# Attention in groups of four heads: the next group's scores and maxima between this group's transposed scores and values

## The reference

```
layer 0:  xn = layernorm(x)
          s  = a recurrence over time with gates (h = tanh(h A + u Bm), y = g (h C' + u D') + (1 - g) xn) W_out + b_out + xn
          g  = silu(tanh(xn wo' + c uo' + bo)),  c from a second recurrence
          x  = x + s * g
layer 1:  xn = layernorm(x)
          q, k, v = xn Wq', xn Wk', xn Wv'            16 heads of 16, scaled by 1/16
          scores  = q k' / 4, causal;  weight = softmax(scores);  s = (weight v) Wproj' / 16
          d2 = squared distances of xn to 32 prototypes; the nearest 2 are chosen, with softmax weights
          g  = silu(sum over the 2 of weight * (A (B xn) + bias))    rank 16
          x  = x + s * g
```

## Time and profile before

| | us |
|---|---|
| median of 3 runs | 1231.76 |
| lowest and highest | 1228.45 and 2604.05 |
| the profiled execution | 1227.31 |
| its span, first to last instruction | 1225.5 |
| first scores of batch 0 | at 456.3 |
| one round of the loop over batches | about 97 |
| mean granted clock of TensorE | 0.936 |

### The profile page before, as it was taken

One profiled execution on the slowest core, in us unless ns is written; L12 is line 12 of the kernel. 1 busy time (PEld: TensorE's weight loads), 2 busy tenths in 40 slices (PEclk: granted clock), 3 DMA queues, 4 the chain that ended last, 5 costly groups with the idle time before them and its releaser, 6 DMA issues.

```text
span 1225.5 us, 20586 instructions
## 1 busy us (share of the span) xinstructions
PE 1069.8 (87%) x6848; PEld 708.9 (58%) x6848; DVE 510.6 (42%) x1028; ACT 488.5 (40%) x1198; POOL 256.6 (21%) x237
## 2 busy tenths in 40 slices
PE   4699999999997557898799799889889889979986
PEld 2267777777775334555555565555555545546644
DVE  4611211212122233644744743653663564565461
ACT  2334444444444202263263264255246336326234
POOL 2200101101004223222321420521322322422000
PEclk8899999999998768899899999989989989989989
DMA  6530101011030075058039019119308506705700
GB/s 212 174 102 29 51 26 51 29 48 49 28 111 18 34 107 99 19 100 159 18 77 181 18 59 153 46 52 129 94 35 128 112 18 112 145 18 93 96 19 18
DMA packets 80501, 93.99 MB, mean 77 GB/s; under 512 B 9920, under 2 KB 72032, under 8 KB 80480
## 3 DMA queue, kind: packets, MB, share of 16 engines
q1 hardware_dynamic: 76256, 89.52, 35.1%
q10 hardware_dynamic: 4224, 4.19, 1.0%
HBM read 59.84 MB, written 33.59 MB: 76 GB/s over the span
## 4 chain that ended last, share of the span: by engine, by line
PE 70%; DVE 10%; issue 7%; ACT 5%; DMA 4%; SPq 2%; POOL 1%; DVEq 0%; ACTq 0%; POOLq 0%
PE PS L708 22%; PE PS L844 5%; PE PS L781 5%; PE PS L922 5%; PE PS L887 5%; DVE nm L1451 5%; PE PS L865 3%; PE PS L695 3%; PE PS L811 3%; PE PS L759 3%; DMA XT<-xt_d 2%; PE PS L948 2%; PE PS L790 2%; PE PS L889 2%; ACT arena L1184 2%
## 5 line engine op out<-in xcount | busy, mean ns | idle before, releaser
L708 PE MATMUL PS<-arena 128*128 128x256 f32 x1024 | 312.1, 421 | 0.0
L1451 DVE TENSOR_REDUCE nm<-PS 128x2 f32<-128x256 f32 (+3 forms) x256 | 200.9, 817 | 90.3 <-PE PS L867 89.3
L695 PEld LDWEIGHTS PS<-arena 128*72 128x72 f32 x1024 | 129.9, 141 | 68.1 <-ACT arena L1069 4.6
L1069 ACT ACTIVATE arena<-PS 64x8 f32<-64x8 f32 x512 | 88.5, 173 | 185.1 <-PE PS L695 181.4
L708 PEld LDWEIGHTS PS<-arena 128*128 128x128 f32 x1024 | 155.5, 192 | 0.0
L865 PE MATMUL PS<-K,Q 96*128 96x128 bf16 (+3 forms) x512 | 129.8, 319 | 25.0 <-DVE nm L1451 20.5
L1184 ACT ACTIVATE arena<-PS 128x1024 f32<-128x1024 f32 x128 | 128.5, 1029 | 29.2 <-PE PS L889 28.6
L887 PE MATMUL PS<-Q,K 98*128 98x512 bf16 (+3 forms) x512 | 122.8, 318 | 16.6 <-DVE nm L1451 14.1
L1311 DVE SCALAR_TENSOR_TENSOR arena<-arena 128x512 f32<-128x512 f32 x16 | 11.1, 694 | 267.7 <-ACT arena L1080 267.7
L695 PE MATMUL PS<-arena 128*72 128x8 f32 x1024 | 121.3, 191 | 0.0
L867 PE MATMUL PS<-negmask,identb 128*128 128x128 bf16 x512 | 105.6, 228 | 0.0
(11 more groups left out here) (161 smaller groups left out, 1399.9 us busy)
## 6 DMA issues: line engine op xcount, KB each, us to landing
qk_d<-QB SPq DMA_DIRECT2D x24, 512.0 KB, 2.9
Q<-qk_d SPq DMA_DIRECT2D x96, 128.0 KB, 8.9
K<-qk_d SPq DMA_DIRECT2D x96, 128.0 KB, 9.5
X<-in_L_attn_x SPq DMA_DIRECT2D x12, 512.0 KB, 13.5
arena<-xt_d SPq DMA_DIRECT2D x16, 256.0 KB, 3.2
gt_d<-arena SPq DMA_DIRECT2D x16, 256.0 KB, 2.5
wx_d<-arena SPq DMA_DIRECT2D x16, 256.0 KB, 2.0
XT<-xt_d SPq DMA_DIRECT2D x8, 512.0 KB, 9.9
```

Of the source, the lines that this page charges most:

```text
L695: pe.matmul(PS[0:WIDE, 7, 0:B], w_ab, HB[:, step], start=True, stop=True).then_inc(c_mm.sem, 1)
L708: mm = pe.matmul(o, lhs, rhs, start=first, stop=last)
L1451: v_.tensor_reduce(nm[:, i, 2 * hp:2 * hp + 2], PS[:, 2 * (u % 3):2 * (u % 3) + 2, 0:(i + 1) * P], AX.X, ALU.max, negate=True).then_inc(m_ ...
```

## The change

Heads go in four groups of four, and a batch is four stages. In stage g TensorE makes the transposed scores of group g in ten units of one bank each, two banks in turn (3 and 4), and between them the scores of the next group in eleven units of one bank each, three banks in turn (0 to 2); group 0 of batch b + 1 is done in stage 3 of batch b. Bank 5 keeps the values, banks 6 and 7 all side steps, now the projection too. The side steps of batches b - 1, b + 1 and b + 2 are spread over the stages. VectorE takes maxima with a reduction for each unit of 512 columns or less, turns into one small piece of 16 rows by 128 per group, writes the scaled values itself (`value`), and does the splits after the maxima of stage 1; ScalarE takes exponentials 512 columns at a time. In DRAM query and key now lie as part, q or k, dimension, head, token; a group's operands are read in six transfers, each of 3, 2 or 1 blocks of 16 rows of four heads (4 KB), where the blocks of the query repeat one part. Before the loop, loads for batch 0 are followed on SP's queue by those for batch 1, and then by the first maxima.

```diff
-PAIRS = [(0, 0), (0, 1), (1, 0), (0, 2), (2, 0), (1, 1)]
+PAIRS = [(0, 0), (0, 1), (0, 2), (1, 0), (1, 1), (2, 0)]
+BLOCKS = [(0, 3), (3, 2), (5, 1)]
 KS = len(PAIRS) * HD
 KM = KS + 2
 SCORE_SCALE = float(D) ** -1.0 * float(HD) ** -0.5
@@ -31,7 +32,13 @@
 P_AT = {0: 0, 1: 512, 3: 896, 2: 1024}
 PU = P_AT[2]
-TU = 3 * H // 2
+G = 4
+GH = H // G
+ROWS = [(3, 0, 1), (3, 1, 1), (3, 2, 1), (3, 3, 1), (2, 0, 1), (2, 1, 1), (2, 2, 1), (2, 3, 1), (1, 0, 2), (1, 2, 2),
+        (0, 0, 4)]
+SU = len(ROWS)
+TQ = 5 * GH // 2
+TU = G * TQ
 PW = NT * (NT + 1) // 2 * P
 BIG = 1.0e30
...
-        qk_d = nc.dram_tensor("qk_d", (SPLIT, 2, D, T), BF16, kind="Internal").ap()
+        qk_d = nc.dram_tensor("qk_d", (SPLIT, 2, HD, H, T), BF16, kind="Internal").ap()
...
+            def save_operands(b, n):
+                if n == 0:
+                    sp.wait_ge(q_ld[G - 1].sem, q_ld[G - 1].at(b, 0))
+                    hold()
+                sp.wait_ge(q_s.sem, q_s.at(b, (2, 5, 6)[n]))
+                for c in range(2):
+                    for m in range(KT):
+                        sp.dma_start(qk_d[n, c, :, m * H // 2:(m + 1) * H // 2].rearrange("d h t -> h d t"),
+                                     QB[:, n, c * KT + m]).then_inc(q_st.sem, 16)
...
+            def load_operands(b, g, after):
+                sp.wait_ge(q_st.sem, q_st.at(b, 2 * KT * SPLIT))
                 hold()
-                if before is not None:
-                    sp.wait_ge(t_mm.sem, t_mm.at(before, (a + 1) * TU // 2))
+                if after:
+                    sp.wait_ge(t_mm.sem, t_mm.at(b - 1, (g + 1) * TQ))
                     hold()
-                rows_of = slice(a * D // 2, (a + 1) * D // 2)
-                heads = slice(a * H // 2, (a + 1) * H // 2)
-                for r, pair in enumerate(PAIRS):
-                    for c, dst in enumerate((Q6, K6)):
-                        sp.dma_start(dst[r * HD:(r + 1) * HD, heads, :],
-                                     qk_d[pair[c], c, rows_of].rearrange("(h d) t -> d h t", d=HD)
-                                     ).then_inc(q_ld[a].sem, 16)
-            def take_maxima(b, a):
-                sp.wait_ge(m_h.sem, m_h.at(b, a + 1))
-                heads = slice(a * H // 2, (a + 1) * H // 2)
-                sp.dma_start(Q6[KS:KS + 1, heads, :], nmh[:, a]).then_inc(m_ld[a].sem, 16)
-                sp.dma_start(Q6[KS + 1:KS + 2, heads, :], nml[:, a]).then_inc(m_ld[a].sem, 16)
-            def batch(b, more):
-                if more:
-                    load_batch(b + 1)
-                take_maxima(b, 0)
+                heads = slice(g * GH, (g + 1) * GH)
+                for at, n in BLOCKS:
+                    first = PAIRS[at][0]
+                    rows_of = slice(at * HD, (at + n) * HD)
+                    sp.dma_start(Q6[rows_of, heads, :],
+                                 qk_d[first:first + 1, 0, :, heads].broadcast_to([n, HD, GH, T])
+                                 ).then_inc(q_ld[g].sem, 16)
+                    sp.dma_start(K6[rows_of, heads, :], qk_d[0:n, 1, :, heads]).then_inc(q_ld[g].sem, 16)
+            def take_maxima(b, g):
+                sp.wait_ge(m_h.sem, m_h.at(b, g + 1))
+                heads = slice(g * GH, (g + 1) * GH)
+                for row, part_of in ((KS, nmh), (KS + 1, nml)):
+                    sp.dma_start(Q6[row:row + 1, heads, :].rearrange("o h (i q) -> o (h i) q", q=P), part_of[:, g]
+                                 ).then_inc(m_ld[g].sem, 16)
...
+            def stage1(b, more, more2):
+                if more2:
+                    load_rows(b + 2)
+                    load_gates(b + 2)
+                take_maxima(b, 2)
+                if more:
+                    save_operands(b + 1, 0)
+            def stage2(b, more):
+                if more:
+                    save_operands(b + 1, 1)
+                    save_operands(b + 1, 2)
+                    load_operands(b + 1, 0, True)
+                    load_operands(b + 1, 1, True)
+                take_maxima(b, 3)
+            def stage3(b, more):
+                if more:
+                    load_operands(b + 1, 2, True)
+                    take_maxima(b + 1, 0)
...
+            def scores(b, g, u):
+                i, h, n = ROWS[u]
+                bank = u % 3
+                if u == 0:
+                    pe.wait_ge(q_ld[g].sem, q_ld[g].at(b, 2 * len(BLOCKS)))
+                elif u == 2:
+                    pe.wait_ge(m_h.sem, m_h.at(b, g))
+                elif u > 2:
+                    pe.wait_ge(m_r.sem, m_r.at(b, g * SU + u - 2))
+                w = (i + 1) * P
+                for e in range(n):
+                    pe.matmul(PS[:, bank, e * w:(e + 1) * w], Q6[0:KS, g * GH + h + e, i * P:(i + 1) * P],
+                              K6[0:KS, g * GH + h + e, 0:w], start=True, stop=False)
+                    mm = pe.matmul(PS[:, bank, (e + 1) * w - P:(e + 1) * w], identb[:, :], negmask[:, :],
                                    start=False, stop=True)
                 mm.then_inc(m_mm.sem, 1)
-            def maxima_turn(b, a, more):
...
+            def turned(b, g, k):
+                if k == 0:
+                    pe.wait_ge(m_ld[g].sem, m_ld[g].at(b, 2))
+                pe.wait_ge(t_e.sem, t_e.at(b, g * TQ + k - 1))
+                h, bank = g * GH + k // 5 * 2 + k % 5 // 2, 3 + k % 2
+                if k % 5 == 4:
+                    turned_tile(b, h - 2, 2, bank, 0)
+                    mm = turned_tile(b, h - 1, 2, bank, 2 * P)
+                elif k % 5 % 2 == 0:
+                    mm = turned_tile(b, h, 0, bank, 0)
+                else:
+                    turned_tile(b, h, 1, bank, 0)
+                    mm = turned_tile(b, h, 3, bank, 3 * P)
...
+            def stage(b, g, side, nxt):
+                for k in range(TQ):
+                    turned(b, g, k)
+                    if nxt is not None:
+                        for u in (2 * k, 2 * k + 1):
+                            if u < SU:
+                                scores(*nxt, u)
+                        if k == 7:
+                            maxima_turn(*nxt)
+                    run(side, k)
...
+            def stage2(b, more):
+                side = {0: [], 1: [lambda: values(b, 1)], 2: [], 3: [lambda: values_turn(b, 1)]}
+                for n, k in enumerate((0, 2, 3, 4, 5, 6, 7, 8)):
+                    side.setdefault(k, []).append(lambda n=n: experts(b, n, more))
+                stage(b, 2, side, (b, 3))
...
+            def maxima(b, g, u):
+                i, h, n = ROWS[u]
+                dve.wait_ge(m_mm.sem, m_mm.at(b, g * SU + u + 1))
+                v_.tensor_reduce(nm[:, g, h:h + n, i],
+                                 PS[:, u % 3, 0:n * (i + 1) * P].rearrange("p (n w) -> p n w", n=n), AX.X, ALU.max,
                                  negate=True).then_inc(m_r.sem, 1)
...
+            def stage(side, nxt):
+                for u in range(SU):
+                    if nxt is not None:
+                        maxima(*nxt, u)
                     for step in side.get(u, ()):
                         step()
-                maxima_low(b, 1)
+                if nxt is not None:
...
+            def stage1(b, more, first=False):
+                side = {6: [lambda: divide(b, 0)]}
+                if not first:
+                    side[1] = [lambda: add_rows(b - 1)]
+                stage(side, (b, 2))
                 if more:
                     split(b + 1, 0, Q)
                     remainder(b + 1, 0)
@@ -1502,25 +1658,31 @@
                     split(b + 1, 1, Q)
                     remainder(b + 1, 1)
                     split(b + 1, 2, Q)
-                    value(b + 1, 0)
-                    value(b + 1, 1)
-                    split(b + 1, 1, K)
-                divide(b, 0)
-                if more:
-                    split(b + 1, 2, K)
                     distance(b + 1)
-                divide(b, 1)
-                if more:
-                    odds_apart(b + 1)
-                    choose(b + 1)
-                divide(b, 2)
-                if more:
-                    weigh(b + 1, 0)
-                    weigh(b + 1, 1)
-                divide(b, 3)
-                if more:
-                    weigh(b + 1, 2)
-                finish(b)
+            def stage2(b, more):
+                side = {6: [lambda: divide(b, 1)]}
+                if more:
+                    side[1] = [lambda: split(b + 1, 1, K)]
+                    side[5] = [lambda: odds_apart(b + 1)]
+                    side[7] = [lambda: split(b + 1, 2, K)]
+                    side[8] = [lambda: choose(b + 1)]
+                side[10] = [lambda: gate(b, 0)]
+                stage(side, (b, 3))
+                gate(b, 1)
```

More of the change, by code:

```diff
@@ L455, in batch, with stage0 @@
+            def stage0(b, more, first=False):
+                if not first:
+                    load_x1(b - 1, more)
+                    load_operands(b, 3, True)
                 if more:
@@ L1009, in _ @@
```

(26 more changed lines are left out.)

715 lines of the change are left out of this document (396 added, 319 removed).

## The result

The changed kernel takes 1460.6 us (median of four, 1458.3 to 1468.5) against 1230.1 before: a ratio of 1.190, 95% interval 1.185 to 1.195. One of the four executions of the kernel before took 2604 us and is left out of the ratio. I had forecast slower, by the right mechanism, with 1410 us and a range up to 1455; the time lies just above it. The profiled execution is the slowest of the four, 1468.5 with a span of 1466.6.

What follows compares the result with a forecast made beforehand. TensorE, with gaps made by waits, was taken to bound the kernel; 81 us of work plus waits and low clock gave a 118.5 us period, and with prologue and last batch 1410 us. Range 1215 to 1455, the forecast's own 1370 to 1455.

Steps and rivals of the forecast that it cites:

- Step 1: VectorE's maxima 28 us a batch (26 before), ScalarE's exponentials about 3 us more, all hidden under TensorE: zero on the sum.
- Step 2: Maxima chain, now four times a period: TensorE waits of 0, 1.4 and 2.5 us behind stages 0, 1 and 3.
- Step 3: Low-rank rounds in stage 3: TensorE waits 2.0 us (0 to 4) for VectorE multiplications standing behind two maxima.
- Step 4: VectorE's 9.9 us block at the end of stage 1: TensorE stands 6.1 us in stage 2 for an unread bank.
- Step 5: Operand loads on 3 and 2 engines in stage 2 hold back group 3's maxima: 18.5 us wait in seven periods.
- Step 6: TensorE's low clock, from gaps of 6 and 18 us: 7 us lost a period (3 to 9), 4.9 before.
- 81: TensorE's own work per batch at 2.4 GHz, in us, taken as the base of the period.
- the 118.5: Forecast period of the batch loop in us, the sum of TensorE's work, waits and low clock, against 97.25 before.
- Loads on 16 engines: Rival: block count does not matter to loads; period 100 to 109, time 1257 to 1337, middle 1295 us; chance 0.17.
- The fed case: Rival, first four steps of stage 2: fast loads, VectorE's block ends in time; period 90.5, 1183 us; chance 0.12.
- The worse case: Rival: loads on few engines also delay SP's issues, so stage 0's maxima come late; over 1455 us; chance 0.05.

Runs made afterwards that it cites:

- interleaved source: Changed kernel with each operand load's source walked with its 16 dimensions outermost and its 3 or 2 blocks inside: 1315.6 us, ratio 1.072.
- the second experiment: Changed kernel with each block of 16 rows loaded as a transfer of its own, 12 per group: 1344.6 us.
- the mended kernel: Changed kernel with loads' 16 dimensions outermost, last cast earlier, VectorE's distances behind it, SP's order and the order before the loop altered: 1209.9 us, ratio 0.987.

## Why the prediction was right in kind and wrong in size

1. **Step 1, sizes:** right. VectorE 55 us a round (52.6 and 2), ScalarE 41 to 43, both hidden.
2. **Step 2, maxima chain:** 1.17 and 1.63 for 1.4 and 2.5, right, the second smaller. But the 0 behind stage 0 is 1.6 to 2.6 in five rounds: the maxima of group 1 go out 7.3 us behind the last load of group 3 and need 5.0 us to land (787.81 to 792.84) instead of 1.7. With interleaved loads this wait is gone, so it is the loads again, in a place where I had put nothing.
3. **Step 3, low rank:** 2.2 for 2.0. Right.
4. **Step 4, VectorE's block:** 5.5 for 6.1. Right.
5. **Step 5, loads in stage 2: the step that failed, by size.** The wait is 25.5 for 18.5. The mechanism is shown by experiment: the engine count by the interleaved source and its marks, the place in the queue by the maxima put first. The count from VectorE's block on (687.3) was 23.6 us to the first load and is 28.4; from there to the landing 22.8 and is 26.0; TensorE's stage ended 1.0 later than I had it. 18.5 + 4.8 + 3.2 - 1.0 = 25.5. Of the 4.8, 1.9 are the length of the cast (next section), 1.7 its start, 1.3 the way from cast to load. Moving the cast took back 7.8 of the wait. The 1.7 have a cause that I had counted only as a lump in step 6: right behind the gap of 5.5 us the clock is low, and the values stand on the way to the cast there. They took 4.26 us where I had put 2.3 (the second line has the granted clock, 0.54, third from the end):

```profile
698.48 4.26 PE L985 MATMUL PS<-arena 128*32 128x512 f32 x32
```

```profile
698.50:702.70 4.20, 4.20 (x34) 1.35 (x34) 1.68 (x3) 0.00 (x0) 3.64 (x2) 0.54 0.31 97
```

Of the 3.2, the rate explains 0.7: I counted 10.6 us a group, and before the loop, where SP is held by the loads alone, a group's last issue follows that of the group ahead by 11.2 and 10.8 (451.88, 463.05, 473.88). The other 2.5 are not rate: beside the data of two groups there are 4.0 us where I had put 1.6, and in the run with the maxima first, where TensorE waits for one group, 4.9 (594.64 to 610.53, less 11.0). What makes them stays open.
6. **Step 6, clock:** 125.5 less 81 and the waits (1.2 + 1.6 + 2.2 + 5.5 + 25.5 + 2.6, and 0.2 in a short one: 38.7) leaves 5.8, for 7. Right.

So this round is 7.0 over the 118.5: 7.0 more for the loads, 2.7 for waits that I had put at 0, and 2.7 less in the other steps. Seven periods of 118.5 less 5.6 were 824; from the start of stage 1 of batch 0 (543.2) to that of batch 7 (1407.3) it is 864. The rest of the 59 us in the span: 3.5 to the first transposed scores (523.2 for 519.7), 3.3 in the first stage 0, 5 in the last batch, and the 6.6 that I took off for overlap, which was not there.

**The range** ended at 1455, and an end that lay 1 us a period higher would have held the time. I had drawn it from the bounds of steps 3, 5 and 6. The bounds of step 5 were two faster rates, so they could only shorten the wait, and the start of the loads, a sum of ten terms, had no bound at all.

**The rivals.** Loads on 16 engines, 1257 to 1337: the run with the interleaved source is that case, 1315.6. The fed case, 1183: the mended kernel comes near it (1209.9), though its reason against stood: VectorE's block had to be moved. The worse case, over 1455, is where the time lies, and in part it is what happened: SP's issues were held (2.0 to 2.4 us) and maxima came late in the stage behind stage 0, but that costs 2.6 us a round at most; the 25.5 at stage 3 are the forecast's own mechanism. The marks count 3, 2 and 16 engines; by the rule of the Trainium skill, "DMA: Bandwidth & Descriptors", section "Why a DMA increments its semaphore by 16 and not by 1", that is what it should be, and here the trace now agrees where both sides differ too. The interleaved loads of 48, 32 and 16 partitions ran at 176 GB/s before the loop, with nothing else under way, and the single blocks of 16 partitions of the second experiment at 131 (last column; the one before is the DMA share):

```profile
444.00:452.00 8.00, 0.00 (x0) 0.00 (x0) 0.00 (x0) 0.00 (x0) 0.00 (x0) 0.50 1.05 176
```

```profile
444.00:460.00 16.00, 0.00 (x0) 0.00 (x0) 0.00 (x0) 0.00 (x0) 0.00 (x0) 0.50 0.97 131
```

All 16 engines were busy, in the first case each at 11 GB/s, where the 3.8 busy ones of the change moved 20 each: four times the busy engines gave 2.3 times the rate. Both have pieces of 4 KB; 16 partitions in pieces of 1 KB ran at 116 in the earlier trace rows. So of the 60 GB/s between 116 and 176 the longer pieces gave 15 at most, and the loads of more partitions the other 45. The Trainium skill, "SBUF — State Buffer", section on the port swizzle, gives 16 adjoining partitions about 109 GB/s; more partitions in a load did go faster here, as it would have it.

**What the new order itself is worth** comes from pairs with the same loads. Interleaved loads: old order 1220.5, the change's order 1315.6, the mended order 1209.9. So between the old order with good loads and the change lie 240 us: 95 by the order as written, 145 by the loads (in the old order the same loads cost 209). With the moves above, the new order gains 11, 0.9%, small but outside the spread of both (1219.6 to 1223.7 and 1208.0 to 1211.9).

## What to carry to other kernels

Read a transfer's outermost dimension, on both sides, as the limit of its number of engines, and count its marks in the trace (one small packet per engine): joining several blocks into one transfer saved six issues and cost 13 of 16 engines. Before a short transfer that the bound engine waits for is put behind long ones on a queue, ask what it costs to put it ahead; here it was ready first. And when the next stage hangs on a chain, put the chain's last small instruction (one cast of 0.7 us) where its engine is idle, and give a range to when the chain starts, not only to how long its transfers take.

## What the runs showed that I had not expected

**VectorE beside GpSimd.** The cast took 2.62 us while a GpSimd addition ran (start, length):

```profile
707.01 2.35 POOL L633 TENSOR_TENSOR SG<-SG,WX 128x1024 f32<-128x1024 f32 x1 [4.21 <-ACT SG L1201]
707.29 2.62 DVE L1503 CAST QB<-QF 128x1024 bf16<-128x1024 f32 x1
```

and 0.69 alone. In the mended kernel the same addition falls on an instruction of 4 columns, usually 0.15 us:

```profile
625.41 2.34 POOL L636 TENSOR_TENSOR SG<-SG,WX 128x1024 f32<-128x1024 f32 x1
```

```profile
625.47 2.30 DVE L1555 TENSOR_TENSOR odds<-near 128x4 f32<-128x4 f32 x1 [0.40 <-POOL near L662]
```

A third place is the remainder of the query at 690.5, which takes 1.23 alone:

```profile
689.98 2.52 POOL L655 TENSOR_TENSOR QF<-QF,QB 128x1024 f32<-128x1024 f32 x1 [9.16 <-DVE QB L1503]
```

```profile
690.53 3.04 DVE L1508 TENSOR_TENSOR QF<-QF,QB 128x1024 f32<-128x1024 f32 x1
```

In all three the VectorE instruction ends behind GpSimd's, by 0.02 to 1.07 us, which is a little less than its own length alone: the price is the rest of GpSimd's instruction, not a factor on VectorE's. It does not hold for every instruction: two maxima of 512 columns, read from PSUM, took 1.28 us together beside a GpSimd remainder (698.90), as they did without one (697.10). With the cast moved away from the addition it took 0.7 in every round, in both runs that moved it alone; that GpSimd's remaining time is the price is read from three places and not tested further.

**A held queue.** With the loads on few engines many of SP's issues take 2.0 to 3.4 us, in the old order once 13 us; with the same number of transfers on 16 engines each takes 0.4 to 0.6. So the slow transfers delay also what stands behind them on SP: in that round of the old order the issues of the next x and its statistics took 9.4 and 10.3 us.
